# Attention with all four score tiles of a step together, probabilities turned into four banks, and k and v projected ahead of q

## The reference

```python
x = x + 0.5 * _L0_ffn_ref(_layernorm(x), ...)     # 8 batches of 512 tokens, 128 wide; 8 experts, top 2
q = einsum('ahe,bce->bach', W_Q, x); k = ...; v = ...   # x layer-normed; 16 heads of 64
scores = einsum('bach,baCh->bacC', k, q)
attn = softmax(where(causal, scores, -1e10) / 8, axis=-1)
z = einsum('bacC,baCh->bach', attn, v)
x = x + einsum('aeh,bach->bce', W_O, z)
x = x + 0.5 * _L0_ffn_ref(_layernorm(x), ...)
```

## Time and profile before

| | us |
|---|---|
| three runs | 1080.07, 1082.15, 1085.09 |
| median | 1082.15 |
| profiled execution, its own time | 1078.47 |
| its span, first to last instruction | 1075.8 |
| TensorE matmul busy | 977.6 (91%) |
| VectorE busy | 841.4 (78%) |
| ScalarE busy | 730.2 (68%) |
| POOL busy | 286.6 (27%) |
| attention, first scores of the first to first scores of the last step | 234.75 to 878.82 |

### The profile page before, as it was taken

How to read it: one execution, slowest core, us unless ns; L and a number is a source line. 1 busy time by engine, 2 the same in 40 slices (tenths; PEclk the granted TensorE clock), 3 DMA queues, 4 the chain that set the end, 5 groups by cost and what they waited for, 6 DMA issues and landing times.

```text
span 1075.8 us, 24556 instructions
## 1 busy us (share of the span) xinstructions
PE 977.6 (91%) x7677; PEld 810.3 (75%) x7677; DVE 841.4 (78%) x3091; ACT 730.2 (68%) x2018; POOL 286.6 (27%) x316
## 2 busy tenths in 40 slices
PE   3567899988999999999999999999999998878994
PEld 2456899876777777777777777777777777768994
DVE  7566788577778788878878878978978888657786
ACT  3334667656877878778778777777777775445672
POOL 3665300223101101321311212210200103555554
PEclk9998999998999999999999999999999999989997
DMA  9234645412112102212112112111111124435576
GB/s 258 79 111 135 204 156 163 148 58 42 30 30 42 36 25 44 38 43 43 35 44 41 36 48 39 38 47 28 44 34 26 43 73 115 127 107 158 174 229 181
DMA packets 90623, 90.23 MB, mean 84 GB/s; under 512 B 30080, under 2 KB 66848, under 8 KB 90496
## 3 DMA queue, kind: packets, MB, share of 16 engines
q1 hardware_dynamic: 77296, 67.79, 22.8%
q0 software_dynamic: 8640, 18.76, 7.3%
q10 hardware_dynamic: 4560, 2.12, 0.7%
HBM read 63.95 MB, written 24.67 MB: 82 GB/s over the span
## 4 chain that ended last, share of the span: by engine, by line
PE 75%; DVE 11%; issue 5%; DMA 3%; another core or an unknown queue 2%; ACT 2%; SPq 1%; POOL 1%; DVEq 0%; ACTq 0%; POOLq 0%
PE psum L1737 12%; PE psum L1767 12%; PE psum L1645 10%; PE psum L1616 7%; PE psum L1614 7%; PE psum L1615 6%; PE psum L1748 6%; PE psum L1752 5%; PE psum L1775 5%; PE psum L1756 2%; PE psum L1623 1%; DVE arena L1350 1%; DVE arena L1369 1%; PE psum L1566 1%
## 5 line engine op out<-in xcount | busy, mean ns | idle before, releaser
L794 ACT ACTIVATE arena<-arena,neg_max 128x512 f32<-128x512 f32 (+3 forms) x512 | 281.0, 551 | 49.6 <-DVE neg_max L1350 44.3
L1350 DVE CUSTOM_DVE_ANT_0 arena<-psum,causal 128x512 f32<-128x512 f32 (+3 forms) x512 | 225.3, 488 | 28.3 <-PE psum L1737 21.9
L752 ACT ACTIVATE arena<-psum,b_t 128x256 f32<-128x256 f32 x312 | 124.1, 477 | 63.2 <-PE psum L1616 43.0
L1645 PE MATMUL psum<-w_sb,arena 128*128 x1248 | 156.9, 279 | 4.6 <-issue 2.2
L1645 PEld LDWEIGHTS psum<-w_sb,arena 128*128 128x128 f32 x1248 | 150.1, 196 | 6.2 <-issue 6.2
L1767 PE MATMUL psum<-arena 128*64 128x512 f32 (+3 forms) x1024 | 152.0, 439 | 0.4 <-DVE arena L1363 0.4
L597 POOL DMA_INDIRECT arena<-y_tiles,y_at x64 | 60.8, 950 | 324.6 <-PE psum L1737 210.0
L578 POOL DMA_INDIRECT x_slots<-xr,slot x64 | 61.9, 967 | 255.6 <-PE psum L1737 212.7
L801 ACT ACTIVATE arena<-psum 128x512 f32<-128x512 f32 x128 | 75.5, 590 | 78.1 <-PE psum L1748 78.1
L1767 PEld LDWEIGHTS psum<-arena 128*64 128x64 f32 x1024 | 68.0, 136 | 77.8 <-issue 59.7
L1363 DVE COPY arena<-psum 128x512 f32<-128x512 f32 x128 | 88.5, 691 | 25.0 <-PE psum L1752 24.1
(11 more groups left out here) (221 smaller groups left out, 2221.6 us busy)
## 6 DMA issues: line engine op xcount, KB each, us to landing
w_raw<-in_L_ffn_W_dram SPq DMA_DIRECT2D x78, 256.0 KB
arena<-inv_dram SPq DMA_DIRECT2D x128, 128.0 KB
xg<-x_slots SPq DMA_DIRECT2D x78, 144.0 KB
y_tiles<-y_sb SPq DMA_DIRECT2D x39, 128.0 KB, 1.7
arena<-y_rows SPq DMA_DIRECT2D x16, 256.0 KB, 3.7
x_slots<-blank SPq DMA_DIRECT2D x18, 144.0 KB
out_dram<-xs ACTq DMA_DIRECT2D x8, 256.0 KB
y_rows<-y_sb,y_tok POOLq DMA_INDIRECT x78
```

Of the source, the lines that this page charges most:

```text
L752: ins = act.activation(h_t[n % 2][:, k, :], H_BANKS[n % 2][k // 2][:, k % 2 * TS:(k % 2 + 1) * TS], ACT.Relu, bias=b1_t[:, bass.ds(e * CHU ...
L794: ins = act.activation(prob_tile(i, h, t), prob_tile(i, h, t), ACT.Exp, scale=-1.0, bias=neg_max[i % 2][:, h, t:t + 1], accum_out=row_sum[ ...
L1350: ins = dve.tensor_tensor_reduce(out=prob_tile(i, h, t), in0=score_tile(t)[:, h, :], in1=causal[:, SEQ - (t + 1) * P:SEQ], scale=-1.0, sca ...
L1645: ins = pe.matmul(Y_BANKS[n % 2][:, r * D:(r + 1) * D], h_t[n % 2][:, k, r * P:(r + 1) * P], w2_sb[:, bass.ds(e * (CHUNKS * D) + k * D, D) ...
```

## The change

Three things are done to attention's lists.
1. **All scores together.** Tiles 1 and 0 move to banks 4 and 5 (`SIDES`), so that all four tiles of a step are computed in one go at its start, before project_out. VectorE takes all maxima in a row; the copies of turned squares no longer stand between.
2. **Squares of both heads turned in one run.** 20 squares make five groups of four: banks 0, 1, 6, 2 and 0 again (`turned_bank`). ScalarE copies groups 0, 2 and 3 (512 columns each, where it was 512, 256, 512, 256), VectorE groups 1 and 4. The two buffers `probs_t` become one of 20 squares. Each group is one run of four transposes with one count of `pt_ps`. The copies are `transposed` on both engines. The last step, whose banks 0 to 3 the next stage uses, has banks 5, 4, 6, 5 and 4.
3. **k, then v, then q.** k's bank is free as soon as tile 2 is read; q's bank holds the fourth group until ScalarE has copied it, so q comes last. Extras stay behind the projections.

The functions called are renamed only in part: `project_qk` is now `project_k` and `project_q` with the same matmuls, `ring_a_taken` has moved and is the same. Waits for `qk_ps` follow the new order. The core of the diff:

```diff
--- before.py
+++ after.py
...
@@
         def pair_cols(i):
             return slice(i % PAIRS * P, (i % PAIRS + 1) * P)
 
-        LONG, SHORT = psum[:, 0:2, :], psum[:, 2:4, :]
+        LONG, SHORT, SIDES = bank[0:2], bank[2:4], bank[4:6]
         RING_A, RING_B, RING_C, O_BANK = bank[4:8]
         Q_BANK, K_BANK = bank[2:4]
...
-        def score_tile(t):
-            both = (LONG, LONG, SHORT, LONG)[t]
-            col = P if t == 1 else 0
-            return both[:, :, col:col + (t + 1) * P]
+        def score_tile(t, h):
+            both = (SIDES, SIDES, SHORT, LONG)[t]
+            col = 2 * P if t == 0 else 0
+            return both[h][:, col:col + (t + 1) * P]
+
+        def turned_bank(i, g):
+
+            if i == STEPS - 1:
+                return (RING_B, RING_A, RING_C, RING_B, RING_A)[g]
+            return (LONG[0], LONG[1], RING_C, Q_BANK, LONG[0])[g]
+
+        def four_turned(g):
+            return probs_t[:, g * 4 * P:(g + 1) * 4 * P]
...
-            def transposed(i, h):
-                act.wait_ge(pt_ps, PT_USES * i + 3 * h + 1)
+            def transposed(i):
                 wait(act, z_ps, i)
-                act.activation(probs_t[h][:, 0:4 * P], RING_A, ACT.Copy).then_inc(pt_act, 1)
-                act.wait_ge(pt_ps, PT_USES * i + 3 * h + 3)
-                act.activation(probs_t[h][:, 8 * P:10 * P], RING_C[:, 0:2 * P], ACT.Copy).then_inc(pt_act, 1)
+                for g in (0, 2, 3):
+                    act.wait_ge(pt_ps, PT_USES * i + g + 1)
+                    act.activation(four_turned(g), turned_bank(i, g), ACT.Copy).then_inc(pt_act, 1)
 
             def attention():
+                take_k(0)
                 take_q(0)
-                take_k(0)
                 for c in range(QT - 1):
                     take_v(c, (RING_A, RING_B)[c % 2])
                 for i in range(STEPS):
                     b, s = divmod(i, PAIRS)
                     if i > 0:
-                        transposed(i - 1, 0)
+                        transposed(i - 1)
                     exps(i, 0, [3])
-                    if i > 0:
-                        transposed(i - 1, 1)
                     if i + 1 < STEPS:
+                        take_k(i + 1)
                         take_q(i + 1)
-                        take_k(i + 1)
                     exps(i, 1, [2])
...
@@
                 yield from normalise(batch_of(0), xa[0], 0, xa_ready)
 
             def attention():
+                split_k(0)
                 split_q(0)
-                split_k(0)
                 work = iter(())
                 for i in range(STEPS):
                     b, s = divmod(i, PAIRS)
                     maxima(i, 0, [3])
                     if i > 0:
                         invert(i - 1)
-                        transposed(i - 1, 0)
                     maxima(i, 1, [2])
+                    maxima(i, 2, [1, 0])
                     if i > 0:
                         transposed(i - 1, 1)
+                        transposed(i - 1, 4)
...
                     go_on(work, 4)
                     if i + 1 < STEPS:
+                        split_k(i + 1)
                         split_q(i + 1)
-                        split_k(i + 1)
                     go_on(work, 2)
-                    maxima(i, 2, [0, 1])
...
-            def transposes(i, h):
...
+            def ring_a_taken(i):
...
+            def transposes(i):
+
+                squares = [(h, k, t) for h in range(2) for k in range(QT) for t in range(k, QT)]
+                for g in range(5):
+                    if i < STEPS - 1:
+                        if g == 0:
+                            pe.wait_ge(max_ready, S_USES * (i + 1) + 1)
+                        if g == 3:
+                            pe.wait_ge(max_ready, S_USES * (i + 1) + 2)
+                        if g == 4:
+                            pe.wait_ge(pt_act, PT_ACT * i + 1)
+                    else:
+                        if g == 1:
+                            ring_a_taken(i)
+                        if g == 2:
+                            pe.wait_ge(z_ready, i)
+                        if g == 3:
+                            pe.wait_ge(pt_act, PT_ACT * i + 1)
+                        if g == 4:
+                            pe.wait_ge(pt_dve, PT_DVE * i + 1)
+                    for n, (h, k, t) in enumerate(squares[4 * g:4 * g + 4]):
+                        col = P_COL[t] + k * P
+                        ins = pe.transpose(turned_bank(i, g)[:, n * P:(n + 1) * P], probs[i % 2][h][:, col:col + P], ident[:, :])
+                    ins.then_inc(pt_ps, 1)
...
-                project_qk(0)
+                project_k(0)
+                project_q(0)
                 for c in range(QT - 1):
                     if c > 1:
                         pe.wait_ge(v_ready, c - 1)
                     project_v(c, (RING_A, RING_B)[c % 2])
                 for i in range(STEPS):
                     b, s = divmod(i, PAIRS)
-                    wait(pe, max_ready, S_USES * i)
                     pe.wait_ge(qk_lo_ready, 2 * (i + 1))
                     scores(i, 3).then_inc(s_ps, 1)
                     scores(i, 2).then_inc(s_ps, 1)
+                    pe.wait_ge(v_ready, min(i + QT - 1, STEPS))
                     if i > 0:
-                        pe.wait_ge(v_ready, min(i + QT - 1, STEPS))
                         ring_a_taken(i - 1)
-                        pe.wait_ge(exp_done, S_USES * i)
-                        wait(pe, z_ready, i - 1)
-                        transposes(i - 1, 0)
+                    scores(i, 1)
+                    scores(i, 0).then_inc(s_ps, 1)
                     if i > 1:
                         project_out(i - 2)
                     if i > 0:
-                        transposes(i - 1, 1)
+                        pe.wait_ge(exp_done, S_USES * i)
+                        transposes(i - 1)
+                    pe.wait_ge(max_ready, S_USES * i + 2)
                     if i + 1 < STEPS:
-                        pe.wait_ge(max_ready, S_USES * i + 2)
-                        project_qk(i + 1)
+                        project_k(i + 1)
+                    pe.wait_ge(max_ready, S_USES * (i + 1))
+                    if i + QT - 1 < STEPS:
+                        project_v(i + QT - 1, RING_B)
+                    wait(pe, pt_act, PT_ACT * i)
+                    if i + 1 < STEPS:
+                        project_q(i + 1)
                     else:
-                        pe.wait_ge(max_ready, S_USES * i + 2)
                         transpose_x(1, 0)
-                    if i + QT - 1 < STEPS:
-                        wait(pe, pt_dve, PT_DVE * i)
-                        if i == 0:
-                            pe.wait_ge(v_ready, QT - 2)
-                        project_v(i + QT - 1, RING_B)
-                    if i > 0:
-                        pe.wait_ge(pt_act, PT_ACT * i)
...
-                    pe.wait_ge(max_ready, S_USES * i + 1)
-                    scores(i, 0)
-                    scores(i, 1).then_inc(s_ps, 1)
                     if i > 0:
                         attend(i - 1)
...
```

91 lines of the change are left out of this document (36 added, 55 removed).

## The result

The changed kernel takes **1073.16 us** (median of 20 runs, 1066.42 to 1077.97), the kernel before 1083.68 in the same comparison (20 runs, 1077.06 to 1091.01): ratio 0.9902, 95% interval 0.9879 to 0.9924. The forecast was 1074.5, with 1065 to 1081 as range. The number came out, and partly by luck: the gain in the scores was twice the forecast, a late copy of ScalarE had not been foreseen, and the term for the first step had the wrong sign. The profiled execution after took 1076.68 us (span 1074.9).

A forecast was written before the change was run, and what follows sets the result against it. TensorE's list per attention step and its waits were taken to bound the kernel. -5.7 - 3.5 + 0.5 + 2.0 = -6.7 from 1082.15 gives 1075.4, less 1 us for a cheaper boundary: 1074.5, range 1065 to 1081.

The forecast's parts named there:

- the term for the first step: Start of attention, pipeline empty: scores after the first step 2.8 us later, some 0.8 given back; +2.0 us.
- What bounds the kernel: Attention steps: TensorE's list, busy 618.3 of 621.4 us; only fewer expensive matmul boundaries and the end of waits can win.
- Boundaries, -5.7: TensorE, each step: v-to-scores and scores-to-attend gone (0.19), q-to-attend new (0.10); 9.93 becomes 9.84, -5.7 us over 63 intervals.
- a tile of scores pays for its first weights wherever it stands: TensorE's scores: moving tiles 1 and 0 behind the others was to leave their first-weight cost unchanged.
- rival 1: q projection to attend is free, or the first step's hold goes; -13.0 or -12.1 us, 1069.5; chance 0.27.
- Division, -3.5 and +0.5: TensorE's waits for VectorE's division, some 16 steps, go: -3.5 us; about 0.5 returns where small VectorE instructions pile up.
- Exps and q: Exps end 2.2 into the next step, 0.9 spare before the transposes; q_lo at 9.05 against 9.84, 0.8 spare.
- rivals 2 and 3: Rival 2: q chain becomes the wait, 1081, chance 0.20. Rival 3: VectorE falls behind with its maxima, 1088, chance 0.08.
- Nothing here binds: Bank reuse in a step: ScalarE's first copy ends at 4.4, TensorE needs the bank at 4.87; no bank makes TensorE wait.
- rival 4: Last stage: whatever holds engines there falls elsewhere; +-3 us on each case, no chance of its own.
- rival 2: q chain's 0.8 us spare is not enough; 0.1 a step, 6.3 us, given as 1075.4 + 6.3 = 1081; chance 0.20.

The follow-up runs named there:

- e5: Changed kernel with project_out moved from behind the scores to between those of tile 1 and tile 0; ratio to the kernel before 1.0060.
- e1: Changed kernel with tile 0's scores issued ahead of tile 1's on TensorE; ratio to the kernel before 0.9933.
- e8: Kernel before with tile 1's scores issued ahead of tile 0's on TensorE; ratio to the kernel before 0.9986.
- e4: Kernel before with TensorE's wait for the division moved from ahead of the first transposes to ahead of their third group; ratio to the kernel before 0.9978.
- e10: Kernel before with six of the eight gathers for the second batch left out; 1027.38 us, on a chip where the kernel before takes 1027.30.
- e9: Changed kernel with six of the eight gathers for the second batch left out; 1012.38 us, on a chip where the kernel before takes 1027.30.
- e13: Changed kernel with six of eight second-batch gathers left out, third run; 1064.03 us, on a chip where the kernel before takes 1076.06.
- e3: Changed kernel with GpSimd's per-step indirect transfers released by the scores of all four tiles, not of tile 3; ratio to the kernel before 0.9897.
- e6: Changed kernel with GpSimd's two indirect transfers of a step released by the end of the q projection, beside attend; ratio to the kernel before 0.9878.
- e7: Changed kernel with gathers of expert results cut to 128 bytes a row from 512; 1015.30 us, where the kernel before takes about 1027.
- e11: Changed kernel with six of the eight gathers for the second batch left out, second run; 1015.03 us beside 1027.36 of the kernel before.

## Why the prediction was right, step by step

**What bounds the kernel.** Right: TensorE is busy 610.51 of 611.23 us, and the instructions are as many as before (7,677 matmuls recorded in either trace; the 6,212 of the prediction stands in neither).

**Boundaries, -5.7.** Right as boundaries: v projection to scores and scores to attend are gone, q projection to attend costs its 0.10, and e5 gives 0.10 and 0.09 for one more way out and in. Wrong was the clause that *a tile of scores pays for its first weights wherever it stands*. Set side by side with the earlier trace rows, a step changes by -0.09 from boundaries, as forecast, -0.16 inside the scores of tiles 1 and 0, and +0.05 in project_out and the transposes (3.10 now, 303.43 to 306.53, 3.05 before): together -0.20, as measured. Of the -0.16, 0.06 is the order of the tiles (e1, e8); the other 0.10 comes of standing right behind tile 2 (tile 1's first pair takes 0.21 behind the v projection in e8 and 0.11 here; e5 pays as much back when project_out stands ahead of tile 0). The term is -12.2 us over 61 intervals, twice the forecast, and equal to what rival 1 had for another reason: its own mechanism, a free way from q to attend, did not happen (0.33, not 0.23). There the trace agrees with the rule that the prediction cited from the Trainium skill's "TensorEngine Tiling (Array Packing)", Key Properties: 128x128 to 128x64 is a change that costs.

**Division, -3.5 and +0.5.** Right in kind; -2.3 by e4. The 16 steps were counted too generously; the waits view's 2.5 was the better reading.

**Exps and q.** Right. In the step at 301.38 ScalarE's last accumulator read ends at 303.20, 1.8 into the step (forecast 2.2). q_lo ends at 310.24, 0.86 ahead of the next scores (forecast 0.8):

```profile
308.95 0.69 DVE L1346 TENSOR_TENSOR k_lo<-psum,k_hi 128x512 fp32r<-128x512 f32 x1 [1.44 <-ACT k_hi L792]
309.56 0.68 DVE L1342 TENSOR_TENSOR q_lo<-psum,q_hi 128x512 fp32r<-128x512 f32 x1
```

The waits view of the 61 intervals has none in front of the scores, and one of 0.2 in front of the transposes; rivals 2 and 3 did not occur.

**Banks: "Nothing here binds".** Wrong, and this is the step that a reader should look at. The fifth bank's release was put at 4.4 and TensorE there at 4.87, with 0.47 to spare, from a row of the place where the copy stood *before*. At its new place GpSimd's transfer delays it by 0.4 to 0.5, just more than the spare: +4.7 us. The trace of before could not show a hold at a moment when ScalarE wanted nothing; but it did show GpSimd's pair in that step, and the argument never asked what it meets after the move.

**The first step, +2.0.** Wrong: -1.5. On the chip that shows no hold the two intervals went from 18.12 (e10) to 16.93 (e9), so the new order alone gains 1.2 us, where the prediction had it cost time. In the profiled pair the clock may play in too (0.85 in that window before, 0.92 now). As for the hold, it neither ended at the same moment nor went. VectorE's maxima escaped it, while the q copy, q_lo and the maxima of step 1 were met by it:

```profile
247.67 0.60 ACT L788 ACTIVATE q_hi<-psum 128x512 fp32r<-128x512 f32 x1 [2.09 <-PE psum L1621]
```

```profile
248.30 0.69 DVE L1342 TENSOR_TENSOR q_lo<-psum,q_hi 128x512 fp32r<-128x512 f32 x1 [1.99 <-issue]
252.02 0.69 DVE L1355 CUSTOM_DVE_ANT_0 arena<-psum,causal 128x512 f32<-128x512 f32 x1 [3.03 <-PE psum L1744]
```

With the gathers out (e13) the two intervals are 3.4 shorter still. The prediction had asked whether instruction fetch holds VectorE, with the Trainium skill's "Runtime: NRT & Kernel Launch", Instruction fetch mechanics, beside it. The runs point to GpSimd: e13 leaves the lists of the other engines as they are, and the two intervals fall to 17.79. What is left above 16.93 was not explained; no run here varies the fetches themselves.

**The last stage, rival 4.** It was called a shift of 3 us either way. The stretch from the last step's scores on is longer in every execution of a kernel with the change than in one without on the same chip: 198.6, 199.7 and 197.1 (e1, e3, e5) against 195.3 (e4); 199.6 (e13) against 197.2 (e8); 174.5 to 176.8 (e6, e7, e9) against 172.8 (e10). So 1.7 to 4.5 us of the gain go there. The traces show where a part of it goes, and it is in attention's own last step, whose waits the prediction did not work out. Its squares go to banks 5, 4, 6, 5 and 4, and the fifth group stands still until VectorE's copy has freed bank 4. TensorE's wait there, in e9:

```profile
PE psum L1787 <- DVE arena L1368: 1.5, 1, 1.5
```

The last matmul of attention's project_out starts 22.08 us behind the last step's first scores in e9, 20.87 in e10: 1.2 of their difference of 1.7. For e13 and e8 it is 22.08 and 21.41, 0.7 of 2.4. In five of the ten executions with the change (the profiled one, e3, e6, e7, e11) the granted clock was 0.50 for 3.4 us right behind this wait, from 889.1 to 892.5 in the profiled one, and the last matmul starts at 23.7, 1.6 later again; in none of the four executions without the change was it low at that place. No run took the wait away. The stage ahead shows no such pattern (first scores at 239.2 to 241.8 against 236.6 on the first of these chips, 235.7 against 234.9 on the second, 212.1 to 212.7 against 214.0 on the third). The rest of the longer last stage stays open.

**The sum.** Attention: -12.2 (steps), -2.3 (division), +4.7 (late copy), -1.5 (start) are -11.3; measured -11.7. Without the late copy the steps and the division should give -14.5 over the 61 intervals; on the chip that shows none it was -13.3 (e9, e10). The forecast's -6.7 came near the measured -10.5 in time because the unforeseen gain in the scores (6.5) was partly eaten by the late copy and by the last stage, while the start did better than feared. That these cancelled is luck. A slip of addition did not matter: rival 2's 1075.4 + 6.3 is 1081.7, not 1081.

## What to carry to other kernels

Price a block by the neighbours that it will have: tiles of matmuls in one run, longest first, hide each other's first weights, and this was worth more here (0.16 a step) than the changes of array shape (0.09). When an engine's instruction moves, look at what all other engines, GpSimd and its transfers among them, are doing at its new time; a spare of half a microsecond worked out from an undisturbed row is not one. Work out the last step by itself where its banks differ from the others'. And an experiment on such a hold tells something only on a chip that shows it.

## What the runs showed of the hardware

- An idle ScalarE starts its copy of a finished bank 0.4 to 0.5 us late when GpSimd's second indirect transfer started 1.3 us before the moment at which the copy is due (36 of 38 steps), and 0.7 late once, where it was 1.0 us before; 0.1 to 0.2 late where it was 1.5 to 1.6 us before (e5), and not late once, where it was 1.8; 0.2 to 0.3 where that was 0.7 us before; not at all where the second starts behind it, even with the first 0.9 us ahead (e3). What is shared was not found.
- This depends on the chip: with the same kernel 34 copies were late on one (the kernel before at 1076 us) and none on two others (about 1027 us). The chips without it are 5% faster as a whole, and nearly all of that lies outside attention: with the same kernel (e9 against e13) the first scores come at 212 against 236 us, the 61 intervals take 607 against 609, and the last stretch 174.5 against 199.6. The granted clock, 0.99 against 0.98 over the whole, differs by too little to explain it.
- A pair of 128-column score matmuls takes 0.06 us behind a longer tile and 0.16 behind a change of array shape, where its weight load starts with it (517.61) and not 0.12 ahead of it (302.94).
